# The last chunk's output projection is taken out of attention's end and spread over the second router's first two turns

## The reference

```
x = x + 0.5 * ffn(layernorm(x))
x = x + attention(layernorm(x))      # 16 query heads of 32, one key/value head
x = x + 0.5 * ffn(layernorm(x))

attention: softmax(q k^T / sqrt(32)) v, heads side by side, then  out @ Wo + bo
ffn:       scores = sigmoid(x @ w_gate); the 6 best of 64 experts, weights divided by their sum,
           at most 256 rows per expert in order of the rows; each expert silu(g) * v, then w_down;
           plus a shared expert for all rows
```

## Time and profile before

| | us |
|---|---|
| median of 3 runs (3119.02 to 3122.38) | 3122.11 |
| the profiled execution's own time | 3151.85 |
| its span, first to last instruction | 3150.1 |
| attention's last matmul on the output weights ends | 2479.5 |
| first DMA of the second router | 2483.24 |
| first DMA of the second experts' stage | 2636.94 |

### The profile page before, as it was taken

One profiled execution on the slowest core, in us unless ns is written; L12 is line 12 of the kernel. 1 busy time (PEld: TensorE's weight loads), 2 busy tenths in 40 slices (PEclk: granted clock), 3 DMA queues, 4 the chain that ended last, 5 costly groups with the idle time before them and its releaser, 6 DMA issues. The chain is left out here.

```text
span 3150.1 us, 44567 instructions
## 1 busy us (share of the span) xinstructions
PE 2751.5 (87%) x15016; PEld 1648.4 (52%) x15016; DVE 2045.3 (65%) x3954; ACT 1523.3 (48%) x2871; POOL 2243.3 (71%) x1461
## 2 busy tenths in 40 slices
PE   7967777489899999999999999999999776888870
PEld 4644444266555555555555555555554474555540
DVE  7843222257788888788788887887874494333334
ACT  5622222153476666566566665765656451222220
POOL 2248888563399979799798897997989323778770
PEclk9979888689999999999999999999999767999995
DMA  5579999895388888799797887987877454999998
GB/s 209 212 208 247 236 237 240 182 287 193 84 183 180 170 179 177 153 194 181 165 184 159 188 166 157 194 173 174 175 149 165 139 211 136 221 234 241 234 183 325
DMA packets 221450, 608.27 MB, mean 193 GB/s; under 512 B 34476, under 2 KB 35500, under 8 KB 193320
## 3 DMA queue, kind: packets, MB, share of 16 engines
q0 software_dynamic: 91760, 376.49, 59.2%
q1 hardware_dynamic: 125240, 220.55, 21.3%
q10 hardware_dynamic: 4224, 8.39, 0.7%
HBM read 230.94 MB, written 155.24 MB: 123 GB/s over the span
## 5 line engine op out<-in xcount | busy, mean ns | idle before, releaser
L1924 DVE TENSOR_REDUCE attention_mx<-attention_pM 128x1 f32<-128x512 f32 x1984 | 1209.3, 682 | 185.1 <-PE attention_pM L1808 184.3
L1755 ACT ACTIVATE attention_prob<-attention_pS 128x512 f32<-128x512 f32 x2048 | 1032.7, 627 | 566.4 <-PE attention_pS L1787 561.7
L1692 POOL TENSOR_TENSOR attention_pair<-attention_prob 128x1024 f32<-128x1024 f32 x380 | 989.8, 2768 | 108.5 <-ACT attention_prob L1755 105.1
L1787 PE MATMUL attention_pS<-attention_qT,prep_kT 128*128 128x512 f32 x2048 | 841.3, 413 | 4.7 <-ACT attention_prob L1755 3.8
L1808 PE MATMUL attention_pM<-prep_kT,attention_qT 96*128 96x512 f32 x1984 | 787.8, 398 | 0.8
L1787 PEld LDWEIGHTS attention_pS<-attention_qT,prep_kT 128*128 128x128 f32 x2048 | 387.3, 189 | 313.0 <-issue 210.2
L768 POOL DMA_INDIRECT sum<-experts_res,c_table x256 | 403.5, 1576 | 124.3 <-issue 82.3
L1836 PE MATMUL attention_pO<-attention_prob,attention_v 128*32 128x512 f32 x4096 | 491.7, 598 | 0.0
L1808 PEld LDWEIGHTS attention_pM<-prep_kT,attention_qT 96*128 96x128 f32 x1984 | 377.9, 190 | 89.3 <-DVE attention_mx L1924 14.4
L752 POOL DMA_INDIRECT experts_rows<-xn_rows,c_table x256 | 250.1, 977 | 104.1 <-issue 74.9
L797 PE MATMUL experts_pT<-c_ident,experts_rows 128*128 128x128 f32 x1024 | 169.8, 307 | 117.1 <-issue 68.0
(11 more groups left out here) (184 smaller groups left out, 3195.3 us busy)
## 6 DMA issues: line engine op xcount, KB each, us to landing
prep_acc<-attention_pair POOLq DMA_DIRECT2D x96, 1024.0 KB, 8.1
attention_acc<-attention_pair POOLq DMA_DIRECT2D x90, 1024.0 KB, 7.7
attention_qT<-q_parts SPq DMA_DIRECT2D x96, 256.0 KB
xn_rows<-route_xn SPq DMA_DIRECT2D x16, 1152.0 KB, 6.6
experts_wup<-in_L_ffn_w_up_dram SPq DMA_DIRECT2D x64, 256.0 KB
q_parts<-prep_acc SPq DMA_DIRECT2D x64, 256.0 KB, 4.3
prep_acc<-prep_acc POOLq DMA_DIRECT2D x16, 1024.0 KB, 7.5
ahead_wup<-in_L_ffn_w_up_dram SPq DMA_DIRECT2D x64, 256.0 KB, 9.1
```

The lines of the kernel that those rows point to most:

```text
L1692: pool.tensor_tensor(to[:, part], prob[2 * n % PROBS][:, part], prob[(2 * n + 1) % PROBS][:, part], ALU.add).then_inc(s_pair, 1)
L1755: act.activation(prob[t % PROBS][:, h * QT:(h + 1) * QT], pS[:, at, :], ACT.Exp).then_inc(s_ex, 1)
L1787: pe.matmul(pS[:, n % 3, :], kT[:, key:key + P], qT[g][:, h, :], start=True, stop=True).then_inc(s_sc, 1)
L1924: dve.tensor_reduce(mx[:, unit, part:part + 1], pM[:, r % RING, :], X, ALU.max).then_inc(s_mr, 1)
```

## The change

Attention ends earlier, and the last chunk's projection becomes work of `route1`:

- In attention PE runs `last_sums(7)` straight behind `last_sums(6)`. ACT copies the sums `pL` to SBUF (`late["d"]`) and DVE copies the last group's `pO` to `o_n[3]`. `last_quarter`, `last_output`, `last_added` and the four stores are gone. `m.close()` is added at the end.
- `route1` on DVE: the reciprocal of `d` (128x512) is its second instruction, ahead of the moments of turn 0. On POOL: `o_n[3] * d` follows the first memset, ahead of turn 0's inverse deviation. On PE: three products (groups 0 to 2) for each of the quarters 0, 1 and 2 come first, those of quarter 3 stand between turn 0's second and third transposed tile, and the four products of group 3 stand between turn 1's transposes and `positions(0)`. They go to four PSUM banks that turn 0 does not use yet. DVE adds the four quarters to `x` behind `select(0)`.
- SP stores the last 512 rows in one DMA of 1 MB behind turn 0's row store, and waits there for DVE's additions. Only turn 7 reads these rows; its load, three turns ahead, waits for the store.
- The tiles that live across the two stages (`o_n`, `wo`, `xo`) are laid in three turns' worth of `kept`, which become its last three turns; the copies of turns 5 and 7 wait until they are free. In the first router and in `project` the same memory is lent to buffers. These change where tiles lie, not what is done with them.

The core of the diff (what is left out are the semaphores' names, the removed functions named above, and the lending of memory):

```diff
 # route, SP
+                    if late and i == 0:
+                        sp.wait_ge(s_late_add, A + TURN)
+                        sp.dma_start(x_view[LATE, :, :, :], late["x"]).then_inc(s_late_st, 16)
 # route, POOL
+                if late:
+                    pool.wait_ge(s_late_rec, A + 1)
+                    pool.tensor_tensor(late["o"][GPC - 1], late["o"][GPC - 1], late["d"][:, :], ALU.mult
+                                       ).then_inc(s_late_on, 1)
 # route, PE
+                def late_output(t, groups):
+                    if GPC - 1 in groups:
+                        pe.wait_ge(s_late_on, A + 1)
+                    for g in groups:
+                        ins = pe.matmul(pLate[t][:, 0:C], late["o"][g][:, t * P:(t + 1) * P], late["wo"][:, g, :],
+                                        start=g == 0, stop=g == GPC - 1)
+                if late:
+                    for t in range(TURN - 1):
+                        late_output(t, range(GPC - 1))
...
+                        if late and i == -1 and j == 1:
+                            late_output(TURN - 1, range(GPC - 1))
+                    if late and i == 0:
+                        for t in range(TURN):
+                            late_output(t, range(GPC - 1, GPC))
 # route, DVE
                 dve.memset(cum[:, :], 0.0).then_inc(s_sel, 1)
+                if late:
+                    dve.reciprocal(late["d"][:, :], late["d"][:, :]).then_inc(s_late_rec, 1)
...
                     if comes(i):
                         select(i)
+                    if late and i == 0:
+                        for t in range(TURN):
+                            late_added(t)
 # attention, ACT
+                act.wait_ge(s_lsum, A + PAIRS)
+                act.activation(late["d"][:, :], pL, ACT.Copy).then_inc(s_late, 1)
+                act.wait_ge(s_late, A + 1)
 # attention, end
+        m.close()
```

More of the change, by code:

```diff
@@ L113, in setup, with route @@
     return k
-def route(nc, tag, k, wts, x_d, xn_d, sums, copy_x, prep=None, later=None, kept=None, first=None):
+def route(nc, tag, k, wts, x_d, xn_d, sums, copy_x, prep=None, later=None, kept=None, first=None,
+          lent=None, late=None):
     w_gate, w_su, w_sd = wts
@@ L138, in route @@
         zero = m.sb("zero", [P, ROW])
-        xt = [m.sb(f"xt{b}", [P, TURN, C]) for b in range(XB)]
+        xt = [m.sb(f"xt{b}", [P, TURN, C]) for b in range(1 if lent else 0, XB)]
+        if lent:
+            xt.insert(0, lent)
         stats = m.sb("stats", [P, 2, TURN, 6])
@@ L225, in tile_T @@
             half = slice(j % HALVES * P, (j % HALVES + 1) * P)
-            return kept[:, (i * TURN + j) // HALVES, :, half]
+            return kept[i][:, j // HALVES, :, half]
         with nc.Block() as block:
@@ L374, in enter @@
                         pe.wait_ge(s_ev, A + i + 1)
+                    if late and t == 0:
+                        pe.wait_ge(s_late_add, A + TURN)
                     pe.wait_ge(s_hot, A + t + 1)
@@ L840, in unit_up @@
                         for c in range(CK):
-                            t = pe.matmul(pU[n % 2][:, v, :], wsu[:, c, o:o + HS], kept[:, u, c, :], start=c == 0,
+                            t = pe.matmul(pU[n % 2][:, v, :], wsu[:, c, o:o + HS], kept[u // 2][:, u % 2, c, :], start=c == 0,
                                           stop=c == CK - 1)
@@ L1113, in project @@
         m = Memory(nc, ctx, tag)
[L1114 removed]
+        got = lent[0:2] + [m.sb(f"got{b}", [P, TURN, C]) for b in range(2, RING)]
         other = [m.sb(f"other{b}", [P, TURN, C]) for b in range(ADDED)]
@@ L1430, in _, with attention @@
                 dve.wait_ge(s_vb, A + NTURN)
-def attention(nc, tag, k, prep, wo, q_d, d_d, sums, xb_d, x_out):
+def attention(nc, tag, k, prep, wo, q_d, d_d, sums, xb_d, x_out, lent, late):
     kT = prep["kT"]
@@ L1500, in attention @@
         o_new = m.sb("o_new", [P, QT])
-        o_n = [m.sb(f"o_n{g}", [P, QT]) for g in range(GPC)]
+        o_n = late["o"]
         d_sb = m.sb("d", [P, QT])
@@ L2030, in program @@
         projections = (wq, bq, wk, bk, wv, bv, wo, bo)
+        top = Memory(nc, ctx, "top")
+        turns = [top.sb(f"turn{i}", [P, HALVES, CK, HALVES * P]) for i in range(3)]
+        flat = [turn[:, :, :, :].rearrange("p u c n -> p (u c n)") for turn in turns]
+        by_tile = [part.rearrange("p (t c) -> p t c", c=C) for part in flat]
+        late = {
+            "o": [flat[0][:, g * QT:(g + 1) * QT] for g in range(GPC)],
+            "wo": by_tile[1],
+            "x": by_tile[2],
+            "d": top.sb("d", [P, QT]),
+        }
         between = ctx.enter_context(ExitStack())
@@ L2033, in program @@
         prep = attention_weights(m)
-        route(nc, "route0", k, gates, x_rows, xn_d, sums[0], True, prep, projections)
+        route(nc, "route0", k, gates, x_rows, xn_d, sums[0], True, prep, projections,
+              lent=by_tile[0])
         prep.update(attention_parts(m))
         experts(nc, "experts0", k, w_up, w_down, xn_d, sums[0], prep)
-        attention(nc, "attention", k, prep, wo, q_d, d_d, sums[0], xb_d, sums[1][0][0:N, :])
+        attention(nc, "attention", k, prep, wo, q_d, d_d, sums[0], xb_d, sums[1][0][0:N, :],
+                  by_tile, late)
         between.close()
         last = Memory(nc, ctx, "last")
-        kept = last.sb("kept", [P, NT // HALVES, CK, HALVES * P])
+        kept = [last.sb(f"kept{i}", [P, HALVES, CK, HALVES * P]) for i in range(NTURN - 3)] + turns
         between = ctx.enter_context(ExitStack())
@@ L2049, in program @@
         }
-        route(nc, "route1", k, gates, sums[1][0][0:N, :], xn_d, sums[1], False, kept=kept, first=first)
+        route(nc, "route1", k, gates, sums[1][0][0:N, :], xn_d, sums[1], False, kept=kept, first=first,
+              late=late)
         experts(nc, "experts1", k, w_up, w_down, xn_d, sums[1], kept=kept, shared=(w_su, w_sd), first=first)
```

104 lines of the change are left out of this document (40 added, 64 removed).

## The result

The changed kernel takes 3110.86 us (median of 6 runs, 3109.84 to 3113.2), the kernel before 3122.24 us on the same chip (6 runs, 3119.02 to 3127.97): a ratio of 0.9959 with a 95% interval of 0.9949 to 0.9969, 11.4 us less where 13.0 were forecast. Its profiled execution took 3111.0 us (span 3109.3). The profiled execution of before was 29.7 us above its median, so the two spans can't be subtracted; what follows compares moments inside the stretch, counted from the last exponential of attention and from S, the second router's first DMA.

A forecast was written before the change was run, and what follows sets the result against it. Attention's end was taken as a serial stretch, the router's turns as bound by DVE. 15.1 us gained less 2.1 lost in turn 0 gave 13.0 off 3122.11: 3109 us, range 3107 to 3112, with rivals 3103 to 3118.

The forecast's parts named there:

- Part 1: Attention's end: earlier last sums, ACT's copy and a cleared barrier bring S 15.1 us earlier, with ends of 14.2 and 16.2.
- The stage's end then costs what the cleared router costs before the experts: Attention's end to the router's first DMA: 1.9 us, taken from the cleared router's row.
- The barrier is not shown for attention with its clear: Attention's end: no row prices this barrier with its clear, so it was bounded by 0.7 to 1.0 and 2.8 us.
- a barrier above 3 us: Attention's end: a sign in the profile after that would show the forecast wrong.
- Part 2: Second router's turn 0: added products and additions, partly paid by PE's clock, make its place reduction 2.1 us later.
- (a): Rival, PE in turn 0: the clock never drops, gain 15.7 us, 3106.4 us; chance 0.20.
- (b): Rival, PE in turns 0 and 1: gate and last four products at the low clock, gain 7.2, 3114.9 us; chance 0.15.
- (c): Rival, PE: low clock from S through the last product, part 1's gain eaten, 3122.3 to 3125.5 us; chance 0.05.
- (d): Rival, attention's end: another wait or longer clear binds it, gain 5.5, 3116.6 us; chance 0.10 with the unforeseen.
- The hidden costs: Turn 0: DVE's reciprocal at most 3.8 us, POOL's multiplication 1.2, late store and turn 4's load, all expected hidden.

The follow-up runs named there:

- e3: Changed kernel with attention's last pair of probabilities added by VectorE instead of GpSimd: 3111.55 us, one run.
- e10: Changed kernel with attention's last pair added by VectorE and no counter clear at attention's end: 3138.23 us, ratio 0.9946 to the kernel before.
- e1: Kernel before with only the counter clear added at attention's end: 3122.41 us, one run.
- e2: Changed kernel without the counter clear at attention's end: 3109.88 us, one run.
- e9: Changed kernel with VectorE adding attention's last pair, no clear, late sums made by TensorE identity products and copied by ScalarE: 3137.83 us, ratio 0.9946 to the kernel before.
- e7: Changed kernel with VectorE adding attention's last pair, no clear, late sums copied by ScalarE and added by GpSimd: 3141.70 us, ratio 0.9957 to the kernel before.
- e4: Changed kernel with all sixteen late products behind turn 1's transposes, none ahead of turn 0's: 3120.21 us, one run.
- e5: Changed kernel with GpSimd issuing nine DMAs in the second router and one in the first: 3142.47 us, one run, beside 3154.36 for the kernel before.
- e6: Changed kernel with the late sums copied by ScalarE and added by GpSimd in turn 1: 3143.44 us, one run.

## Why the prediction was right, step by step

**Part 1, right in mechanism, one term too small.** The last sums started 5.76 us behind the start of GpSimd's last pair (forecast 5.86), ACT's copy ended at 7.46 (7.74), without a table load before it. The term that failed is "The stage's end then costs what the cleared router costs before the experts", 1.9, with its bounds of 0.7 and 2.8: it measured 4.46. The row behind it was of a stage whose end waits for no drain of GpSimd; e3 puts this stage in that condition and gets 1.84, e10 without the clear 1.04, so both prices were right for what they priced. The prediction had named "a barrier above 3 us" as a sign of being wrong, and for this term it was. "The barrier is not shown for attention with its clear" was taken for a question of the clear alone; the clear is 0.82 us (e1, e2), and the other 2.6 are GpSimd's drain, which could be read ahead of the change in the rows of the barrier's line. The gain of part 1 was 12.86, not 15.1, and below the 14.2 that was its lower end.

**Part 2, right in pattern, too dear by 1.7 us.** The place reduction was forecast 2.1 us late and is 0.42 late. The clock did what was forecast: low at first, high for the gate, though PE had idled 5.77 us ahead of its first product and not the 2.7 of the forecast, since the barrier was longer. Three products ran low, not four, and one at the high clock is 0.86 us apart, not 0.93, so the gate started at S + 16.17 (forecast 17.3), took 3.79 (3.7), and ACT's table load, ending at 2482.27, set the scores at S + 20.23 (21.5). The last four products ran at the high clock behind transposes that did so too (the working had given these transposes the low clock's price, 3.5 us, behind a gate at the high clock: ended at S + 25.0, measured 22.4), and ended 0.7 us before VectorE's first addition (2486.83 + 1.02 against 2488.55); `positions(0)` was at S + 25.64, not 28.7. The additions cost 0.60 each, not 0.69, and of their 2.4 us only 1.8 show: from mask to place reduction it is 6.91 us (5.14 before), since before VectorE stood ready for GpSimd's product there. In e9, without them, it is 5.09. So +1.8 of additions and -1.35 of earlier scores make the 0.42.

**The two errors met.** Part 1 gave 2.2 too little, part 2 1.7 too much: 12.4 against 13.0. That the median came within 2 us of the forecast is partly this, and luck.

**The rivals.** (a), the clock never drops, did not occur: every profile of the kernel after has its first products at the low clock, and in e7, e9 and e10, where PE had idled only 2.3 to 2.5 us, the clock fell too (4.51 us for the first three products, against 2.74 at the high clock). (b), the gate low, occurred in part in e10 and wholly in e4, whose products are elsewhere. (c) is refuted by the windows. (d) named "another wait" or "a longer clear": another wait it was, 2.6 us of GpSimd's drain, and not the clear; (d) had priced it at half of part 1. The hidden costs stayed hidden: VectorE's reciprocal took 3.35 us (at most 3.8), and moments began at S + 4.04 against 3.89; GpSimd's product took 1.27; the late store waited only for the additions (issued at 2491.05, landed in 5.8 us), and turn 4's load behind it landed 8.8 us after its issue, with two turns to spare.

**The clock's phase.** In three executions of the kernel after, the first three products took 5.31, 5.22 and 5.33 us, and in e5 and e6, whose barrier is the same, 4.98 and 5.38; in five variants whose barrier ends at another moment (e2, e3, e7, e9, e10) 4.41, 5.46, 4.51, 4.51 and 4.51, and e10's gate 4.83 where the others had 3.79. The Trainium skill's rule of a free-running gate ("TensorE: Matmul & The Clock Gate", Part 1) fits the variants, which differ as if by where the drop and rise fall; the executions with the same barrier show a small spread, and the runs' own spread did not grow as the prediction had taken from the rule (3.4 us over six runs, 9.0 before).

## What to carry to other kernels

When a change strips the end of a stage down, look at what every engine's drain does at that barrier, not only at the last store: a drain hidden under 14 us of other work is a term of the sum once that work is gone. Here it paid to let GpSimd, whose drain was long, finish first. And ask what work handed away from a saturated VectorE will run beside: given to GpSimd it came back, 3.0 us for 1.7, while on TensorE and ScalarE it cost turn 1 nothing. A gain of 3 us inside a stretch need not show in the median of five runs of 3140 us: compare the moments as well.

## What had not been expected of the hardware

GpSimd's drain ended 5.5 us behind its last operation in attention, in every kernel, with 217 DMAs issued by it, and 0.2 and 0.86 us behind it after one and nine. A clear of the stage's counters with its own barrier costs 0.82 us. Four additions of 128x512 on GpSimd in 6.44 us lengthened three of VectorE's operations beside them, the shortest sevenfold (0.18 to 1.24 us), and left others as they were.
